# Moving a last copy across a stage boundary, swapping two small steps, and letting the last bank of a feed-forward lag five blocks

## The chip, the cores and the metric

The kernel runs on one core of a Trainium2 chip. The metric is the device time of one execution in microseconds (us); lower is better. Times of before come from three runs and one profiled execution.

## The reference, cut to what matters

One block of a perceiver on 16 batches of 64 tokens (1024 tokens, 512 channels) with a context of 16 x 1601 rows:

```
x = x + xattn(layernorm(x), ctx)      # 16 heads of 32, softmax over 1601 context rows
x = x + attn(layernorm(x))            # 16 heads of 32, 64 tokens per batch, alibi bias
h = square(relu(layernorm(x) @ W_fc.T))        # 512 -> 2048
y = h @ W_proj.T                               # 2048 -> 512
x = x + (spikes of a neuron driven by y in 5 steps) / 5
```

Every product is made in three matmul passes (high x high, low x high, high x low), where a float32 value is split into a high part that ScalarE rounds and a low part, the difference, that VectorE makes.

## The kernel before, in words

There are three stages, each a block of per-engine programs, with a boundary between them at which all engines meet: `prologue`, `cross_attention`, and `attention_and_feed_forward`. Within a stage the order on each engine is written out by hand, and semaphores join the engines. All DMAs are issued by SyncE (SP) on one queue.

**The prologue** (line 187) normalises x, turns it, and multiplies by Wq in eight query units n = 0 to 7 (four blocks of 128 output rows by two halves of 512 tokens), each 12 matmuls of 512 columns into one of four banks of `s_ps` (`q_bank[n % 4]`). ScalarE copies each unit to `xs` in `query(n)` (line 318), and SP stores it to HBM (`q_scratch`) in lines 235 to 238. ScalarE also splits the four quarters of the first batch's context, which VectorE completes. The last instruction of ScalarE is `query(7)`, the last of SP the store of unit 7.

**The cross-attention** (line 395) goes through 16 batches. SP first loads Wv (1024 KB), waits for all eight stores (`q_out`, line 517), loads the first batch's queries `q_sb` (128 KB), then the leftover context rows (`y_left`, 2304 KB), then the next batch's context. TensorE computes keys in units of 12 matmuls of 402 columns into a ring of three banks; ScalarE copies each to `k_sb[:, i % 2]`. The first scores (line 919), which read `q_sb`, follow the fifth key unit. The first write to `k_sb[:, 1]` is the copy of that fifth unit.

**The self-attention** is in the third stage. Its TensorE program is written out in lines 1770 to 1835. `qk(u)` makes 12 matmuls of 512 columns, into the same bank `ring_bank` for u from 10 on, so that each waits for ScalarE's copy of the one before (`qk_out`); `transposes(t, n)` turns half of the probabilities of token tile t into `t_bank` (4 matmuls), ScalarE's `copy` takes them out; `weigh(t)` multiplies them by the values (64 small matmuls), ScalarE's `high(t)` and VectorE's `low(t)` take the result out.

**The feed-forward** (loop at line 1837) has 48 blocks: 16 blocks of 128 hidden rows for each of three groups of token tiles, of 4, 2 and 2 tiles. In step m of the loop TensorE runs `hidden(m)` (12 matmuls, 256 columns in the last two groups), then `project(m - 3, ...)`, which is 3 matmuls of 512 columns per token tile. In the last group (blocks 32 to 47) the two tiles are parted: the first tile's bank is `project(m - 3)` and the last tile's bank is `project(m - 3 - LAG)`, with LAG = 3. So the loop goes on for 3 + LAG steps after the last `hidden`, and the last tile is finished LAG steps behind the first.

A block's values go through: `hidden(n)` on TensorE, relu on ScalarE (line 1435), square on VectorE (line 1515), the high part on ScalarE (`hidden_high`, line 1361), the low part on VectorE (`hidden_low`, line 1521), `project(n)` on TensorE. In the last group the high and low parts have six places (HS = 3 places of double width): the place of block n is that of block n - 6. `hidden_high(n)` therefore waits for `y_part`, which counts the blocks whose *last* bank is done:

```
        def h_before(n):
            return n - HS if n < ALL - FB + HS else n - 2 * HS
                act.wait_ge(sq_ok, n + 1)
                reached(act, y_part, h_before(n) + 1)
```

ScalarE's order in its step m is relu(m), `hidden_high(m - 1)`, and in steps 40 to 42 also `weights(19)` to `weights(21)` (line 1355), the high part of three weight blocks that are loaded anew; GpSimd makes their low parts (line 1319). VectorE's order is square(m), up to two neuron operations of earlier tiles, `hidden_low(m - 1)`. At the end VectorE runs six neuron operations for each of the last two tiles in a fixed interleaving (lines 1620 to 1633): four of the first tile (line 1489 once, 1493 three times), then the first of the last tile, which waits for the very last matmul, and so on; two stores of x end the program.

Of the kernel before, what the change touches and what calls it, by code (L numbers as in the profile page):

```python
# [8 lines left out]
ACT = mybir.ActivationFunctionType  # L9
# [6 lines left out]
P = 128  # L16
DC = D // P
MP = M + M % 2
TOK = B * N
TT = TOK // P  # L20
# [6 lines left out]
NBLK = H * DH // P  # L27
# [143 lines left out]
class Shared:  # L171


    def __init__(self, nc, ctx, context):
        sb = lambda n, s, d=F32: ctx.enter_context(nc.sbuf_tensor(n, s, d))
        sem = lambda n: ctx.enter_context(nc.semaphore(n))
        with ExitStack() as late:
            self.w_late = late.enter_context(nc.sbuf_tensor("w_late", [P, DC, D], F32))
        self.wk_s, self.wv_s = context.keep, sb("wv_s", [P, 2, DC, D], F32R)
        self.k_sb = sb("k_sb", [P, 2, MK])  # L180
        self.context = context
        self.y_in = [sem(f"y_in{q}") for q in range(KC)]
        self.y_hi_ok, self.y_lo_ok = sem("y_hi_ok"), sem("y_lo_ok")
        self.q_out = sem("q_out")


def prologue(nc, x, yT, wq, wk, q_dram, sh, ident, ones, s_ps):
# [4 lines left out]
    with ctx:  # L192
        sb = lambda n, s, d=F32: ctx.enter_context(nc.sbuf_tensor(n, s, d))
        sem = lambda n: ctx.enter_context(nc.semaphore(n))
        HALF = TT // 2
        HT = HALF * P
        NQ = NBLK * 2
# [3 lines left out]
        xs = sb("p_x", [P, TT, D])  # L201
# [9 lines left out]
        wq_in, wk_in = sem("p_wq_in"), sem("p_wk_in")  # L211
        ident_ok, ln_step, var_ok, root_ok, xn_ok = sem("p_ident"), sem("p_ln_step"), sem("p_var"), sem("p_root"), sem("p_xn")
        turned, xt_hi, xt_lo = sem("p_turned"), sem("p_xt_hi"), sem("p_xt_lo")
        q_ps, q_ok, wq_hi, wq_lo, wk_hi = sem("p_q_ps"), sem("p_q_ok"), sem("p_wq_hi"), sem("p_wq_lo"), sem("p_wk_hi")
        block = ctx.enter_context(nc.Block())

        def half_of(n):
# [2 lines left out]
        @block.sync  # L220
        def _(sp):
            def rows(n):
                at = slice(n * PAIR * P, (n + 1) * PAIR * P)
                sp.dma_start(xs[:, n * PAIR:(n + 1) * PAIR], x[at].rearrange("(t p) d -> p t d", p=P)).then_inc(x_in[n], 16)

            rows(0)
            rows(1)
            sp.dma_start(wq_raw[:], wq.rearrange("(c p) e -> p c e", p=P)).then_inc(wq_in, 16)
            rows(2)
            rows(3)  # L230
            sp.dma_start(wk_raw[:], wk.rearrange("(c p) e -> p c e", p=P)).then_inc(wk_in, 16)
# [3 lines left out]
            for n in range(NQ):  # L235
                half, i = half_of(n)
                sp.wait_ge(q_ok, n + 1)
# [67 lines left out]
        @block.scalar  # L305
        def _(act):
            def root(half):
                at = slice(half * HALF, (half + 1) * HALF)
                act.wait_ge(var_ok, half + 1)
                act.activation(ve[:, 1, at], ve[:, 0, at], ACT.Sqrt).then_inc(root_ok, 1)  # L310

            def high(half):
                for t in range(half * HALF, (half + 1) * HALF):
                    act.wait_ge(turned, t + 1)
                    act.activation(xnT[:, 0, :, t * P:(t + 1) * P],
                                   t_ps[t % 4][:].rearrange("p (c q) -> p c q", c=DC), ACT.Copy).then_inc(xt_hi, 1)

            def query(n):
                act.wait_ge(q_ps, n + 1)
                act.activation(xs[:, n, :], q_bank[n % 4], ACT.Copy).then_inc(q_ok, 1)  # L320
# [12 lines left out]
            query(0)  # L333
            query(1)
            query(2)
            high(1)
            context_high(0)
            query(3)
            for n in range(NBLK, NQ):
                if n - NBLK + 1 < KC:  # L340
                    context_high(n - NBLK + 1)
                query(n)

        @block.tensor
        def _(pe):
# [14 lines left out]
            def first_queries(units):  # L360

                pe.wait_ge(wq_hi, 1)
                pe.wait_ge(xt_hi, HALF)
                for n in units:
                    for c in range(DC):
                        product(n, c, 0, 0, start=(c == 0))
                pe.wait_ge(wq_lo, 1)
                for n in units:
                    for c in range(DC):
                        product(n, c, 1, 0)  # L370
                pe.wait_ge(xt_lo, HALF)
                for n in units:
                    for c in range(DC):
                        mm = product(n, c, 0, 1, stop=(c == DC - 1))
                    mm.then_inc(q_ps, 1)

            def queries(units):
                for n in units:
                    half, i = half_of(n)
                    pe.wait_ge(xt_lo, HALF * (half + 1))  # L380
                    if n >= 4:
                        pe.wait_ge(q_ok, n - 3)
                    three_passes(pe, q_bank[n % 4], lambda a, c: wq_s[:, a, c, i * P:(i + 1) * P],
                                 lambda a, c: xnT[:, a, c, half * HT:(half + 1) * HT]).then_inc(q_ps, 1)

            pe.wait_ge(ident_ok, 2)
            for n in range(WARM):
# [7 lines left out]
def cross_attention(nc, x, yT, y_left, v_left, q_dram, o_dram, wv, wp, bp, awq, sh, ident, ones, s_ps):  # L395
# [10 lines left out]
    with ctx:  # L406
# [73 lines left out]
        def _(sp):  # L480
# [33 lines left out]
                load_left(b + 1)  # L514

            sp.dma_start(wv_raw, wv.rearrange("(c p) e -> p c e", p=P)).then_inc(wv_in, 16)
            sp.wait_ge(sh.q_out, 16 * 2 * NBLK)
            load_q(0)
            sp.dma_start(left_rows, y_left).then_inc(left_in, 16)
# [52 lines left out]
        def _(act):  # L572
# [49 lines left out]
            def value_weights():  # L622
                act.wait_ge(wv_in, 16)
                act.activation(sh.wv_s[:, 0], wv_raw, ACT.Copy).then_inc(wv_hi, 1)

            def keys_phase(b, past=True):
                for c in range(KC):
                    key(b, 0, c)
                if not past:
                    value_weights()  # L630
                for i in range(1, NBLK):
                    key(b, i, 0)
                    score(b, i - 1, 0)
# [19 lines left out]
            def values_phase(b, more):  # L653
# [29 lines left out]
                else:  # L683
                    gather(2)

            keys_phase(0, False)
            values_phase(0, True)
            with act.Fori(1, B - 1) as b:
# [418 lines left out]
def attention_and_feed_forward(nc, x, attn_w, attn_b, wo, bo, alibi, w_ffn, context, x_sb, xnT, ident, out, s_ps):  # L1107
# [23 lines left out]
    LOADS = FB + MISSING * (len(GROUPS) - 1)  # L1131
    LEAD = 3
    HALF = OutputAndNorm.HALF
    AHEAD, LAG = 3, 3
    EARLY = 1
    QK = 2 * NBLK * 2
    ctx = ExitStack()
    with ctx:
# [499 lines left out]
        def _(pe):  # L1638
# [150 lines left out]
            transposes(0, 1)  # L1789
            scores(3)  # L1790
            qk(12)
            weigh(0)
            transposes(1, 0)
            qk(13)
            transposes(1, 1)
            qk(14)
            weigh(1)
            transposes(2, 0)
            qk(15)
            transposes(2, 1)  # L1800
            value(2)
# [112 lines left out]
```

## Time and profile before

| what | value |
|---|---|
| median of 3 runs | 1810.27 us (1810.23 to 1812.09) |
| the profiled execution's own time | 1810.56 us |
| its span | 1808.8 us |
| TensorE busy | 1791.4 us, 99% of the span |
| VectorE, ScalarE, GpSimd busy | 1306.2, 827.4, 898.4 us |
| granted TensorE clock, mean | 0.999 of full speed |

The span is what the profiler saw between the first and the last instruction; the execution's own time is 1.8 us longer. The end of a matmul in this profile is modelled, so a TensorE that is shown busy is not one at its peak. A timeline row gives start, duration, engine, line, operation and tiles, the count of merged instructions, and in brackets the idle time before it and what ended it. PEld is TensorE's weight load, which may run ahead of the matmul before it.

### The profile page before, as it was taken

The numbers are of one execution on the slowest core, as the hardware profiler recorded it, in microseconds if no ns is written. First come the engines' busy times: TensorE is split into PE (matmuls) and PEld (weight loads), VectorE is DVE, ScalarE is ACT, GpSimd is POOL, SyncE is SP. The second block draws the span as 40 slices with busy tenths as digits, with TensorE's granted clock in tenths as the row PEclk, the third lists the DMA queues.
The fourth block names the chain that finished last, engine by engine and source line by source line (L and its number), as shares of the span: only waits on it lengthen the run. The fifth ranks groups of instructions, "written<-read, shape, count | busy, mean of one in ns | idle before, by whom it ended". The sixth has DMA issues, their size and how long they took to land. (4 is left out here: it accounts for less than half of the span.)

```text
span 1808.8 us, 65801 instructions
## 1 busy us (share of the span) xinstructions
PE 1791.4 (99%) x28780; PEld 1557.7 (86%) x28780; DVE 1306.2 (72%) x1942; ACT 827.4 (46%) x982; POOL 898.4 (50%) x824
## 2 busy tenths in 40 slices
PE   8999999999999999999999999999999999999998
PEld 7979898989898989898989888888888887778887
DVE  6865959595969686877778686869696967574265
ACT  4634545454545454444445444545453524344232
POOL 0343737373737373737364646465555654344111
PEclk9999999999999999999999999999999999999999
DMA  6210202020202020202020201111020232123110
GB/s 254 112 54 3 84 3 83 4 83 3 84 3 83 4 83 3 83 3 84 3 83 9 78 21 66 42 45 65 22 83 3 76 114 69 26 91 107 37 59 24
DMA packets 43359, 101.20 MB, mean 56 GB/s; under 512 B 19120, under 2 KB 20656, under 8 KB 42960
## 3 DMA queue, kind: packets, MB, share of 16 engines
q1 hardware_dynamic: 43088, 96.88, 15.2%
q8 instruction: 256, 4.19, 0.9%
q14 instruction: 15, 0.12, 0.0%
HBM read 86.48 MB, written 8.29 MB: 52 GB/s over the span
## 5 line engine op out<-in xcount | busy, mean ns | idle before, releaser
L556 POOL TENSOR_TENSOR fold<-fold,prob 128x256 f32<-128x256 f32 x698 | 705.9, 1011 | 55.2
L114 PE MATMUL ring<-y_parts,w_keep 128*128 128x402 f32 (+1 forms) x3072 | 607.7, 351 | 1.5 <-PEq L192 1.4
L114 PEld LDWEIGHTS ring<-y_parts,w_keep 128*128 128x128 f32 x3072 | 551.4, 188 | 16.2 <-issue 3.1
L114 PE MATMUL ring<-wv_s,y_parts 128*128 128x512 f32 x2304 | 545.1, 395 | 0.0
L114 PEld LDWEIGHTS ring<-wv_s,y_parts 128*128 128x128 f32 x2304 | 430.7, 188 | 98.7
L550 POOL TENSOR_TENSOR fold<-prob 128x256 f32<-128x256 f32 x64 | 80.4, 1256 | 623.4 <-ACT prob L610 623.4
L579 ACT ACTIVATE k_sb<-ring 128x402 f32<-128x402 f32 (+1 forms) x256 | 129.4, 506 | 362.3 <-PE ring L114 362.3
L770 DVE TENSOR_TENSOR prob<-prob,peak_rows 128x1024 f32<-128x1024 f32 (+1 forms) x192 | 261.7, 1416 | 1.6
L604 ACT ACTIVATE prob<-s_ps 128x1536 f32<-128x1536 f32 (+1 forms) x128 | 200.0, 1562 | 127.8 <-PE s_ps L919 127.8
L735 DVE TENSOR_TENSOR fold<-fold,prob 128x512 f32<-128x512 f32 x192 | 173.0, 901 | 79.6 <-ACT prob L604 73.9
L610 ACT ACTIVATE prob<-prob 128x1024 f32<-128x1024 f32 (+1 forms) x192 | 210.9, 1125 | 7.4 <-DVE prob L770 5.1
L919 PEld LDWEIGHTS s_ps<-q_sb,k_sb 32*64 32x64 f32 x13312 | 156.2, 130 | 37.5 <-issue 37.3
L919 PE MATMUL s_ps<-q_sb,k_sb 32*64 32x64 f32 x13312 | 173.9, 231 | 0.0
L788 DVE TENSOR_TENSOR y_parts<-y_raw,y_parts 128x1608 fp32r<-128x1608 f32 (+1 forms) x60 | 123.8, 2084 | 35.7 <-ACT y_parts L615 35.7
L587 ACT ACTIVATE v_sb<-ring 128x512 f32<-128x512 f32 x96 | 57.4, 598 | 193.1 <-PE ring L114 193.1
L728 DVE TENSOR_TENSOR fold<-prob 128x512 f32<-128x512 f32 x64 | 52.8, 825 | 128.3 <-ACT prob L604 128.3
L615 ACT ACTIVATE y_parts<-y_raw 128x1608 fp32r<-128x1608 f32 (+1 forms) x60 | 92.4, 1540 | 32.8 <-PE ring L114 32.8
L938 PEld LDWEIGHTS small_ps<-prob,v_sb 128*32 128x32 f32 (+1 forms) x6344 | 91.5, 110 | 16.6 <-issue 16.6
L938 PE MATMUL small_ps<-prob,v_sb 128*32 128x64 f32 (+1 forms) x6344 | 101.4, 220 | 0.0
L707 DVE COPY v_sb<-ring 128x512 f32<-128x512 f32 x96 | 65.0, 677 | 15.5 <-PE ring L114 15.5
L762 DVE COPY peak<-peak 32x8 f32<-32x8 f32 x192 | 63.0, 328 | 6.2
L1319 POOL TENSOR_TENSOR y_parts<-f_raw,y_parts 128x1024 fp32r<-128x1024 f32 x12 | 30.1, 2519 | 73.7 <-ACT y_parts L1355 73.5
(214 smaller groups left out, 1622.2 us busy)
## 6 DMA issues: line engine op xcount, KB each, us to landing
y_raw<-yT SPq DMA_DIRECT2D x48, 804.0 KB, 7.1
y_raw<-yT SPq DMA_DIRECT2D x16, 792.0 KB, 9.9
f_raw<-w_ffn SPq DMA_DIRECT2D x22, 512.0 KB, 3.6
v_sb<-y_left SPq DMA_DIRECT2D x1, 2304.0 KB, 11.3
v_sb<-v_left SPq DMA_DIRECT2D x16, 130.0 KB
p_x<-x SPq DMA_DIRECT2D x4, 512.0 KB, 6.5
q_scratch<-p_x SPq DMA_DIRECT2D x8, 256.0 KB, 2.1
q_sb<-q_scratch SPq DMA_DIRECT2D x16, 128.0 KB, 9.2
```

The costliest lines, as they stand in the source:

```text
L114: mm = pe.matmul(out, left(a, c), right(b, c), start=(c == 0 and n == 0), stop=(c == DC - 1 and n == 2))
L550: pool.tensor_tensor(acc, prob[:, i, 0, :], prob[:, i, 1, :], ALU.add).then_inc(sum_step, 1)
L556: pool.tensor_tensor(acc[0:m], acc[0:m], prob[0:m, i, t, :], ALU.add).then_inc(sum_step, 1)
L579: act.activation(k_sb[:, i % 2, at:at + w], bank(unit)[:, 0:w], ACT.Copy).then_inc(act_out, 1)
L604: act.activation(prob[:, i, a:z, :].rearrange("p t (g q) -> p t g q", g=HB), s_ps[:, :, 0:(z - a) * N].rearrange("p g (t q) -> p t g q", q=N),
L610: act.activation(piece(i, n), piece(i, n), ACT.Exp, scale=SCALE).then_inc(exp_ok, 1)
L615: act.activation(y.part(0, q), y.quarter(q), ACT.Copy).then_inc(y_hi_ok, 1)
L735: dve.tensor_tensor(wide(i), wide(i), prob[:, i, t:t + 2, :], ALU.max).then_inc(tree, 1)
L770: dve.tensor_tensor(piece(i, n), piece(i, n), row(n), ALU.subtract).then_inc(sub_ok, 1)
L788: dve.tensor_tensor(y.part(1, q), y.quarter(q), y.part(0, q).bitcast(F32), ALU.subtract).then_inc(y_lo_ok, 1)
L919: mm = pe.matmul(s_ps[side * N:(side + 1) * N, g, (t - a) * N:(t - a + 1) * N], k_sb[rows, i % 2, at:at + N], q_sb[rows, i, :], start=True ...
L938: pe.matmul(at[g * DH:(g + 1) * DH, 0:N], v_sb[0:m, t, (HB * i + g) * DH:(HB * i + g + 1) * DH], prob[0:m, i, t, g * N:(g + 1) * N], start ...
```

## The change

It does three things. The copy of query unit 7 leaves the prologue: ScalarE makes it as its first instruction of the cross-attention, into the unused second half of `k_sb`; SP stores it there, behind the load of Wv; and ScalarE waits for all stores before it writes that half of `k_sb`. In the self-attention `transposes(1, 0)` is put ahead of `weigh(0)` and `transposes(2, 0)` ahead of `weigh(1)`. LAG in the feed-forward becomes 5.

```
@@ class Shared
-        self.q_out = sem("q_out")
+        self.q_out, self.q_ps, self.q_ok = sem("q_out"), sem("p_q_ps"), sem("p_q_ok")
+        self.last_q = self.k_sb[:, 1, 0:TT // 2 * P]
@@ prologue, SP  (q_ps and q_ok are sh.q_ps and sh.q_ok from here on)
-            for n in range(NQ):
+            for n in range(NQ - 1):
                 half, i = half_of(n)
-                sp.wait_ge(q_ok, n + 1)
+                sp.wait_ge(sh.q_ok, n + 1)
                 sp.dma_start(q_dram[:, i, half * HT:(half + 1) * HT], xs[:, n]).then_inc(sh.q_out, 16)
@@ prologue, ScalarE
             for n in range(NBLK, NQ):
                 if n - NBLK + 1 < KC:
                     context_high(n - NBLK + 1)
-                query(n)
+                if n < NQ - 1:
+                    query(n)
@@ cross_attention, SP
             sp.dma_start(wv_raw, wv.rearrange("(c p) e -> p c e", p=P)).then_inc(wv_in, 16)
+            sp.wait_ge(sh.q_ok, 2 * NBLK)
+            sp.dma_start(q_dram[:, NBLK - 1, TOK // 2:], sh.last_q).then_inc(sh.q_out, 16)
             sp.wait_ge(sh.q_out, 16 * 2 * NBLK)
             load_q(0)
@@ cross_attention, ScalarE
+            def last_queries():
+                act.wait_ge(sh.q_ps, 2 * NBLK)
+                act.activation(sh.last_q, s_ps[:, NBLK - 1, :], ACT.Copy).then_inc(sh.q_ok, 1)
+
             def keys_phase(b, past=True):
                 for c in range(KC):
                     key(b, 0, c)
                 if not past:
                     value_weights()
+                    act.wait_ge(sh.q_out, 16 * 2 * NBLK)
                 for i in range(1, NBLK):
...
+            last_queries()
             keys_phase(0, False)
@@ attention_and_feed_forward
-    AHEAD, LAG = 3, 3
+    AHEAD, LAG = 3, 5
@@ attention_and_feed_forward, TensorE
             qk(12)
+            transposes(1, 0)
             weigh(0)
-            transposes(1, 0)
             qk(13)
             transposes(1, 1)
             qk(14)
+            transposes(2, 0)
             weigh(1)
-            transposes(2, 0)
             qk(15)
```

## Rows read from the trace of the kernel before

**Rows 1.** The page: busy time by engine.

```profile
PE 1791.4 (99%) x28780; PEld 1557.7 (86%) x28780; DVE 1306.2 (72%) x1942; ACT 827.4 (46%) x982; POOL 898.4 (50%) x824
```

**Rows 2.** Timeline at the boundary behind the prologue: start, duration, engine, line, what.

```profile
23.23 13.86 PE L114 MATMUL s_ps<-p_xnT,p_wq 128*128 128x512 f32 x60
...
37.12 0.60 ACT L320 ACTIVATE p_x<-s_ps 128x512 f32<-128x512 f32 x1 [2.12 <-PE s_ps L114]
...
38.52 11.23 PE L114 MATMUL ring<-y_parts,w_keep 128*128 128x402 f32 x60 [1.44 <-PEq L192]
```

**Rows 3.** Timeline at the boundary behind the cross-attention, TensorE.

```profile
1481.62 3.06 PE L987 MATMUL s_ps<-w_keep,y_parts 128*128 128x512 f32 x12
...
1484.99 3.04 PE L114 MATMUL ring_bank<-w_keep,y_parts 128*128 128x512 f32 x12 [0.30 <-PEq L406]
```

**Rows 4.** DMA issues from 38 to 60 us: KB each, us to landing; then the first scores.

```profile
v_sb<-xwv SPq DMA_DIRECT2D x1, 1024.0 KB, 5.7
q_scratch<-p_x SPq DMA_DIRECT2D x1, 256.0 KB, 2.1
q_sb<-q_scratch SPq DMA_DIRECT2D x1, 128.0 KB, 4.9
...
49.68 1.25 PE L919 MATMUL s_ps<-q_sb,k_sb 32*64 32x64 f32 x96
```

**Rows 5.** Timeline of the self-attention, TensorE.

```profile
1545.56 3.05 PE L114 MATMUL ring_bank<-xnT,y_parts 128*128 128x512 f32 x12
1548.54 0.26 PE L1718 MATMUL o_banks<-y_raw 64*32 64x64 f32 x4
...
1549.33 0.66 PE L1701 MATMUL t_bank<-ident,sa_chain 128*128 128x128 f32 x4
1549.74 3.03 PE L114 MATMUL ring_bank<-xnT,y_parts 128*128 128x512 f32 x12
1552.60 0.60 PE L1701 MATMUL t_bank<-ident,sa_chain 128*128 128x128 f32 x4
1553.63 3.02 PE L114 MATMUL ring_bank<-xnT,y_parts 128*128 128x512 f32 x12 [0.43 <-ACT kT L1330]
```

**Rows 6.** Timeline of the feed-forward's last blocks and end.

```profile
1793.17 1.57 PE L1760 MATMUL s_ps<-y_parts,f_h 128*128 128x512 f32 x6
...
1794.35 0.65 PEld L1760 LDWEIGHTS s_ps<-f_w,f_h 128*128 128x128 f32 x3
...
1794.84 0.42 ACT L1361 ACTIVATE f_h<-y_raw 128x256 fp32r<-128x256 f32 x1 [0.77 <-PE s_ps L1760]
...
1795.29 0.43 DVE L1521 TENSOR_TENSOR f_h<-y_raw,f_h 128x256 fp32r<-128x256 f32 x1 [0.74 <-ACT f_h L1361]
...
1798.74 2.23 PE L1760 MATMUL s_ps<-f_w,f_h 128*128 128x512 f32 x9
...
1801.03 0.68 DVE L1489 TENSOR_SCALAR y_raw<-s_ps 128x512 f32<-128x512 f32 x1
```

**Rows 7.** Timeline: a projection that had waited for VectorE's low part.

```profile
1741.21 0.41 DVE L1521 TENSOR_TENSOR f_h<-y_raw,f_h 128x256 fp32r<-128x256 f32 x1
...
1741.67 1.23 PEld L1760 LDWEIGHTS s_ps<-w_keep,f_h 128*128 128x128 f32 x6 [0.63 <-DVE f_h L1521]
```

**Rows 8.** Feed-forward steps 40 to 43: ScalarE's and GpSimd's weights, projections; line 1319.

```profile
1774.27 1.05 ACT L1355 ACTIVATE f_w<-f_raw 128x1024 fp32r<-128x1024 f32 x1
...
1775.40 5.46 POOL L1319 TENSOR_TENSOR f_w<-f_raw,f_w 128x1024 fp32r<-128x1024 f32 x2 [35.59 <-ACT f_w L1355]
...
1779.78 0.86 PE L1760 MATMUL s_ps<-f_w,f_h 128*128 128x512 f32 x3
1780.05 1.09 DVE L1521 TENSOR_TENSOR f_h<-y_raw,f_h 128x256 fp32r<-128x256 f32 x1
...
1781.77 0.53 PEld L1760 LDWEIGHTS s_ps<-y_parts,f_h 128*128 128x128 f32 x3
...
L1319 POOL TENSOR_TENSOR f_w<-f_raw,f_w x3: 2402/2588/2916, 1775.4 to 1781.0; 128x1024 fp32r<-128x1024 f32 x3
```

More of the change, by code:

```diff
@@ L183, in __init__ @@
         self.y_hi_ok, self.y_lo_ok = sem("y_hi_ok"), sem("y_lo_ok")
-        self.q_out = sem("q_out")
+        self.q_out, self.q_ps, self.q_ok = sem("q_out"), sem("p_q_ps"), sem("p_q_ok")
+        self.last_q = self.k_sb[:, 1, 0:TT // 2 * P]
 def prologue(nc, x, yT, wq, wk, q_dram, sh, ident, ones, s_ps):
@@ L213, in prologue @@
         turned, xt_hi, xt_lo = sem("p_turned"), sem("p_xt_hi"), sem("p_xt_lo")
-        q_ps, q_ok, wq_hi, wq_lo, wk_hi = sem("p_q_ps"), sem("p_q_ok"), sem("p_wq_hi"), sem("p_wq_lo"), sem("p_wk_hi")
+        wq_hi, wq_lo, wk_hi = sem("p_wq_hi"), sem("p_wq_lo"), sem("p_wk_hi")
         block = ctx.enter_context(nc.Block())
@@ L234, in _ @@
                 sp.dma_start(y.raw[:, DC * at:DC * (at + w)], yT[0, :, DC * at:DC * (at + w)]).then_inc(sh.y_in[q], 16)
-            for n in range(NQ):
+            for n in range(NQ - 1):
                 half, i = half_of(n)
-                sp.wait_ge(q_ok, n + 1)
+                sp.wait_ge(sh.q_ok, n + 1)
                 sp.dma_start(q_dram[:, i, half * HT:(half + 1) * HT], xs[:, n]).then_inc(sh.q_out, 16)
@@ L318, in query @@
             def query(n):
-                act.wait_ge(q_ps, n + 1)
-                act.activation(xs[:, n, :], q_bank[n % 4], ACT.Copy).then_inc(q_ok, 1)
+                act.wait_ge(sh.q_ps, n + 1)
+                act.activation(xs[:, n, :], q_bank[n % 4], ACT.Copy).then_inc(sh.q_ok, 1)
             def context_high(q):
@@ L341, in _ @@
                     context_high(n - NBLK + 1)
-                query(n)
+                if n < NQ - 1:
+                    query(n)
         @block.tensor
@@ L374, in first_queries @@
                         mm = product(n, c, 0, 1, stop=(c == DC - 1))
-                    mm.then_inc(q_ps, 1)
+                    mm.then_inc(sh.q_ps, 1)
             def queries(units):
@@ L381, in queries @@
                     if n >= 4:
-                        pe.wait_ge(q_ok, n - 3)
+                        pe.wait_ge(sh.q_ok, n - 3)
                     three_passes(pe, q_bank[n % 4], lambda a, c: wq_s[:, a, c, i * P:(i + 1) * P],
-                                 lambda a, c: xnT[:, a, c, half * HT:(half + 1) * HT]).then_inc(q_ps, 1)
+                                 lambda a, c: xnT[:, a, c, half * HT:(half + 1) * HT]).then_inc(sh.q_ps, 1)
             pe.wait_ge(ident_ok, 2)
@@ L516, in _ @@
             sp.dma_start(wv_raw, wv.rearrange("(c p) e -> p c e", p=P)).then_inc(wv_in, 16)
+            sp.wait_ge(sh.q_ok, 2 * NBLK)
+            sp.dma_start(q_dram[:, NBLK - 1, TOK // 2:], sh.last_q).then_inc(sh.q_out, 16)
             sp.wait_ge(sh.q_out, 16 * 2 * NBLK)
@@ L624, in value_weights, with last_queries @@
                 act.activation(sh.wv_s[:, 0], wv_raw, ACT.Copy).then_inc(wv_hi, 1)
+            def last_queries():
+                act.wait_ge(sh.q_ps, 2 * NBLK)
+                act.activation(sh.last_q, s_ps[:, NBLK - 1, :], ACT.Copy).then_inc(sh.q_ok, 1)
             def keys_phase(b, past=True):
@@ L630, in keys_phase @@
                     value_weights()
+                    act.wait_ge(sh.q_out, 16 * 2 * NBLK)
                 for i in range(1, NBLK):
@@ L684, in values_phase @@
                     gather(2)
+            last_queries()
             keys_phase(0, False)
@@ L1133, in attention_and_feed_forward @@
     HALF = OutputAndNorm.HALF
-    AHEAD, LAG = 3, 3
+    AHEAD, LAG = 3, 5
     EARLY = 1
@@ L1791, in _ @@
             qk(12)
+            transposes(1, 0)
             weigh(0)
-            transposes(1, 0)
             qk(13)
@@ L1796, in _ @@
             qk(14)
+            transposes(2, 0)
             weigh(1)
-            transposes(2, 0)
             qk(15)
```

## The prediction

> **What bounds the kernel now.** I read the page first, then the timeline at the three places that the change touches. TensorE is busy 99% of the span [rows 1] and no other engine over 72%, so only what opens or closes an idle stretch of TensorE counts, besides what follows its last matmul. The first such place is the boundary behind the prologue: the last query matmul ends at 37.09 (23.23 + 13.86) and the next stage's first starts at 38.52, 1.44 us idle. ScalarE's copy of query unit 7 lies inside that gap, 37.12 to 37.72, and SP's store follows it [rows 2]. The second is the self-attention around `weigh(0)`, the third the last 16 blocks of the feed-forward and the end [rows 5 to 8].
>
> **A, the copy and store of unit 7.** Removed from ahead of the boundary: one 0.60 us copy and one store. TensorE is then the last engine to arrive. The boundary behind the cross-attention shows that case: last matmul ends 1484.68, next starts 1484.99, idle 0.30 [rows 3]. So A gains 1.44 - 0.30 = 1.14 us. Bounds: 0.84 (a gap of 0.6 stays, twice the other boundary's) to 1.3 (a gap near 0.1); I take 1.14, from the nearest row. Added behind the boundary: the same copy, first on ScalarE, which otherwise has nothing until the first key unit; nothing waits behind it. On SP the store and the wait for it now stand between the Wv load and `load_q(0)`. The Wv load lands 5.7 us after its issue, a store alone 2.1, and `q_sb`, issued behind Wv, landed after 4.9 [rows 4]. If the store waits out Wv it has landed by 5.7 + 2.1 = 7.8 us after the boundary, and `q_sb`, with an empty queue, some 2.1 later, at about 10. TensorE wants it at 49.68 - 38.52 = 11.2 us [rows 2, 4]. So it costs 0, with little over 1 us of cover; it is a rival below. The leftover rows and the next context are issued up to 6 us later than before on the same queue; they are read by ScalarE and VectorE after the first scores, and TensorE's wait for them lies further still; 0. ScalarE's new wait stands where ScalarE comes some 10 us after the boundary, when the stores are in: 0.
>
> The Trainium skill (DMA: Bandwidth & Descriptors, section Queues, rings and completion order) says that descriptors of one queue are consumed in ring order and that a semaphore increment lands only after every earlier write of that DMA engine. By it the store lands behind Wv and not after 2.1 us. The landing of `q_sb` at 4.9, when Wv was ahead of it, agrees.
>
> **B, the two swaps.** The same instructions, another order. Now: `qk(12)` starts 1545.56, the weighing 1548.54, the turn 1549.33, `qk(13)` 1549.74, 4.18 us in all. In the new order the turn follows a `qk`, which takes 2.86 us as at `qk(13)` (1549.74 to 1552.60); the weighing starts when the turn's 0.60 are over, and the next `qk` 0.79 after it as the turn did: 4.25 [rows 5]. So +0.07 at the dearest; a turn that is overlapped at its end by the next matmul would make it -0.1. Two swaps: 0, bounds -0.2 to +0.2. What the swap brings, a turned half that ScalarE copies 0.9 us sooner, nobody waits for; what TensorE does wait for is ScalarE's copy of the `qk` bank, 0.43 us ahead of `qk(14)` [rows 5], and that bank and the single turn that covers its copy are as before.
>
> **C, LAG 5.** The number of matmuls is the same: two blocks' last-bank projections leave steps 38 and 39 and come behind the old end. The dependence is not the same. `hidden_high(n)` waits for the last bank of block n - 6, which is now run in step n - 6 + 3 + 5 = n + 2, at that step's very end; the first bank of block n is wanted in step n + 3. With LAG 3 it was step n, three steps ahead. So the chain *end of a projection, high part, low part, next projection* now turns once a step. Its length from rows: the matmul ends at e = 1793.17 + 1.57 = 1794.74, the high part starts 0.10 later (1794.84), the low part 0.45 after that (1795.29), lasts 0.43 [rows 6], and a weight load started 0.05 behind a low part that it waited for [rows 7]. Sum: e + 1.03.
>
> *Steps 48, 49, 50* have no `hidden`; each first-bank projection (blocks 45, 46, 47) follows directly on the last-bank projection for which its own high part waits. Without the wait its weight load starts at 1794.35 = e - 0.39 [rows 6]. So each is delayed by 1.03 + 0.39 = 1.42 us, and three by 4.26. Bounds: 1.32 each if the first 0.10 is nothing, 1.55 each if TensorE picks up again slower, 4.0 to 4.7 in all.
>
> The Trainium skill (Perfetto Trace Analysis, section Tensor Engine Instruction) says that the end of a matmul in the profile is computed and not observed. By it the 0.10 is soft; with 0 in its place the three would cost 4.0. No row here shows a matmul's true end.
>
> *Steps 41 to 47* (blocks 38 to 44) have a `hidden` between. After e = 1779.78 + 0.86 = 1780.64 the next projection's weight load starts at 1781.77, e + 1.13 [rows 8]. The chain is ready at e + 1.03: hidden, by 0.10 us. I take 0 for these; if the chain is longer by 0.2 to 0.4, seven steps cost 0.7 to 2.1.
>
> *GpSimd in that stretch.* A low part that starts under GpSimd's line 1319 does not end before it: the second of its operations ended at 1775.40 + 5.46 = 1780.86, and the low part begun at 1780.05 took 1.09 and ended at 1781.14, 0.28 behind [rows 8]. Now nobody waits for that; with LAG 5 TensorE does. `weights(19)` to `weights(21)` stand behind `hidden_high(39)`, (40), (41), so they now start some 0.45 after the end of steps 41, 42, 43; GpSimd follows 1.13 after ScalarE's start (1774.27 to 1775.40) and takes 2.40 (the shortest of the three) [rows 8]: it ends at 0.45 + 1.13 + 2.40 = 3.98. A step is 1.13 to the next projection's weight load, 1.57 for the six matmuls of both projections [rows 6] and, as an estimate, a tenth for the load's lead: 2.8. So GpSimd ends 1.18 into the next step; the low part ends at 1.46, the weight load starts at 1.51 instead of 1.13: 0.4 late. Then the step is longer (3.2), the second operation ends 0.8 into the following one and the chain's own 1.03 rules; the third is as the first. Two delays: +0.8, bounds 0 (GpSimd early by half a microsecond) to 1.6 (three at 0.5).
>
> *The end.* The first tile's bank is done two blocks (1.4 us) sooner relative to TensorE's end, so VectorE's four operations on it are over before it. But VectorE's first operation on the last tile starts at 1801.03 already, and the last matmul ends at 1798.74 + 2.23 = 1800.97 [rows 6]: it waits for TensorE and not for those four. From there the eight operations stand in the same order. Gain 0.0 to 0.1; I take 0.
>
> **The sum.** -1.14 + 0 + 4.26 + 0.8 = +3.9 us. Against the profiled execution's own 1810.56 that is 1814.5; the median of the runs shown is 0.3 lower, so I predict 1814.2. Its own bounds: -1.3 - 0.2 + 4.0 + 0 = +2.5 to -0.84 + 0.2 + 4.7 + 1.6 = +5.7.
>
> **The rivals.**
> 1. *Not slower.* Only A acts: the three waits at the end don't open because a high part is let go earlier than I read (the place would have to be free one projection sooner). Price: 1810.3 - 1.1 = 1809.1. It decides where C's sum is under 1.14, that is under 0.4 us per wait. Against it: the wait names block n - 6 and `y_part` counts last banks alone. 0.10.
> 2. *The seven covered steps open too*: the margin of 0.10 us is within the softness of a modelled end. About 0.2 each, +1.4: 1815.6. For it: the margin; against: TensorE's pick-up after VectorE was 0.05 in the one row. 0.17.
> 3. *The boundary keeps its gap*: another engine's arrival or the jump to new code holds it at 1.4; +1.1: 1815.3. Against: the 0.30 of the other boundary. 0.08.
> 4. *The first scores wait for `q_sb`*: store 7.8 us, then a load of 4.9 as measured in a busy queue, 12.7 against 11.2: +1.5, 1815.7. 0.05.
> 5. *A's and C's terms both smaller*, the chain overlapped better than the rows let see, 1 us per wait and nothing from GpSimd: +1.9, 1812.2. 0.05.
>
> **How the numbers follow.** The forecast has 0.55. A measurement of this kernel can tell about 0.2%, 3.6 us, from no change: 1813.9 is the line, and the forecast lies just beyond it. Of its 0.55 I give 0.31 above and 0.24 below. Slower: 0.31 + 0.17 + 0.08 + 0.05 = 0.61; faster by over 3.6 us would need rival 1 and a gain that I don't see: 0.02; the rest, 0.37, within. The range takes the forecast's bounds nearly whole, reaches over rivals 2 to 4, and leaves out rival 1 and rival 5: 1812.5 to 1816.8.
>
> **What would show it.** At the boundary: TensorE's first key matmul with 0.3 idle instead of 1.44, ScalarE's copy behind it, `q_sb` landed before the first scores, which show no wait for a DMA. In the self-attention: the same 0.43 ahead of `qk(14)`. In the last group: ScalarE's high parts waiting for TensorE's line 1760 once a step; a low part stretched under GpSimd and TensorE waiting for it twice; after the last `hidden` three waits of TensorE on VectorE's line 1521 with about 1 us of idle each; VectorE's line 1489 for the last tile right behind the last matmul. The prediction is wrong if those three waits are missing, if the seven covered steps show idle of their own, or if the boundary still has over 1 us.

## The result, and the profile after

| | before | changed |
|---|---|---|
| median of 16 runs each, same chip | 1810.37 us (1810.06 to 1813.58) | 1814.10 us (1813.75 to 1816.68) |
| ratio, with its 95% interval | | 1.0020 (1.0013 to 1.0028) |
| profiled execution's own time | 1810.56 us | 1814.45 us |
| its span | 1808.8 us | 1812.6 us |

The changed kernel is 3.7 us slower; the interval of the ratio makes this 2.4 to 5.1 us. The forecast of 1814.2 was 0.1 us above the measured median. The two profiled spans differ by 3.8 us, so the profile shows what the medians show, and the mean granted clock is 0.999 in both.

First the page's busy time by engine, of the changed kernel (to hold against [rows 1]).

```profile
PE 1793.6 (99%) x28780; PEld 1558.9 (86%) x28780; DVE 1305.5 (72%) x1942; ACT 827.8 (46%) x982; POOL 898.6 (50%) x824
```

The counts are the same to the instruction: nothing was added to any engine's work. TensorE is still shown busy 99% of the span. A loss of 4 us in 1810 can't be seen here, and TensorE's busy time even rose by 2.2 us. The places that the change touches have to be read one by one.

**The boundary behind the prologue** (answers to [rows 2]). Timeline of the changed kernel: start, duration, engine, line, what; in brackets the idle time before it. Line numbers of the changed kernel are up to 10 higher than those of before; ScalarE's copy is now line 632.

```profile
37.56 0.39 SPq L518 DMA_DIRECT2D v_sb<-xwv  x1
...
37.58 0.60 ACT L632 ACTIVATE k_sb<-s_ps 128x512 f32<-128x512 f32 x1 [2.38 <-PEq L193]
37.61 11.24 PE L114 MATMUL ring<-y_parts,w_keep 128*128 128x402 f32 x60 [0.32 <-PEq L193]
38.21 0.33 SPq L520 DMA_DIRECT2D q_scratch<-k_sb  x1
...
43.89 0.69 SPq L490 DMA_DIRECT2D q_sb<-q_scratch  x1
...
48.78 1.25 PE L929 MATMUL s_ps<-q_sb,k_sb 32*64 32x64 f32 x96
```

TensorE is idle for 0.32 us instead of 1.44, and ScalarE's copy of unit 7 now runs beside its first key matmuls. The price is on SP's queue. The view of the DMA issues from 37 to 60 us (KB each, us from issue to landing; answers to [rows 4]) has it:

```profile
v_sb<-xwv SPq DMA_DIRECT2D x1, 1024.0 KB, 5.6
...
q_scratch<-k_sb SPq DMA_DIRECT2D x1, 256.0 KB, 5.7
q_sb<-q_scratch SPq DMA_DIRECT2D x1, 128.0 KB, 2.7
```

The store took 2.1 us when it was issued ahead of the Wv load. Behind it, it takes 5.7 and lands when Wv has. Only then does SP issue the load of `q_sb` (43.89), which lands at 43.89 + 2.7 = 46.6. The first scores start at 48.78 and their row names no wait: 2.2 us of cover, the time between the landing and the first use, are left.

**The self-attention** (answers to [rows 5]). Timeline of TensorE in the changed kernel:

```profile
1544.66 3.05 PE L114 MATMUL ring_bank<-xnT,y_parts 128*128 128x512 f32 x12
1547.55 0.60 PE L1711 MATMUL t_bank<-ident,sa_chain 128*128 128x128 f32 x4
1548.08 0.26 PE L1728 MATMUL o_banks<-y_raw 64*32 64x64 f32 x4
...
1548.87 3.05 PE L114 MATMUL ring_bank<-xnT,y_parts 128*128 128x512 f32 x12
...
1552.79 3.01 PE L114 MATMUL ring_bank<-xnT,y_parts 128*128 128x512 f32 x12 [0.43 <-ACT kT L1340]
```

From `qk(12)` to `qk(13)` it is 4.21 us, against 4.18. The 0.43 us ahead of `qk(14)` stand as before. Over both swaps, from `qk(12)` to `qk(15)`, it is 12.29 us (1544.66 to 1556.95) against 12.23 (1545.56 to 1557.79).

**The feed-forward.** The waits view of the changed kernel from 1760 us to the end (engine, buffer, line, what it waited for: us in total, times, longest):

```profile
ACT f_h L1371 <- PE s_ps L1770: 20.1, 10, 3.2
DVE f_h L1531 <- ACT f_h L1371: 16.7, 10, 2.6
...
PEld s_ps L1770 <- DVE f_h L1531: 5.0, 5, 1.5
...
PE s_ps L1770 <- DVE f_h L1531: 3.1, 3, 1.0
```

The same view of before has ScalarE's high part waiting for TensorE once (0.8 us), VectorE's low part once (0.7 us), and no row of TensorE waiting for a low part.

So the loop from a projection through ScalarE and VectorE back to TensorE is closed in ten steps, and TensorE's weight load is late in five of them. Two of the five lie under GpSimd. Timeline of the changed kernel, steps 40 to 43 (answers to [rows 8]):

```profile
1777.34 2.41 POOL L1329 TENSOR_TENSOR f_w<-f_raw,f_w 128x1024 fp32r<-128x1024 f32 x1 [38.22 <-ACT f_w L1365]
...
1777.72 0.86 PE L1770 MATMUL s_ps<-f_w,f_h 128*128 128x512 f32 x3
...
1779.12 0.90 DVE L1531 TENSOR_TENSOR f_h<-y_raw,f_h 128x256 fp32r<-128x256 f32 x1 [1.10 <-ACT f_h L1371]
...
1780.08 0.53 PEld L1770 LDWEIGHTS s_ps<-y_parts,f_h 128*128 128x128 f32 x3 [0.31 <-DVE f_h L1531]
...
1780.88 0.86 PE L1770 MATMUL s_ps<-f_w,f_h 128*128 128x512 f32 x3
...
1782.87 0.53 PEld L1770 LDWEIGHTS s_ps<-y_parts,f_h 128*128 128x128 f32 x3
...
1786.02 0.53 PEld L1770 LDWEIGHTS s_ps<-y_parts,f_h 128*128 128x128 f32 x3 [0.26 <-DVE f_h L1531]
```

The low part lasts 0.90 us instead of 0.43 and ends at 1780.02, 0.27 behind GpSimd's end (1777.34 + 2.41 = 1779.75). The load behind it starts 1780.08 - (1777.72 + 0.86) = 1.50 us after the projection before it ended. In the following step, where GpSimd has ended early enough, it is 1782.87 - 1781.74 = 1.13, and one step later late again.

The other three stand behind the last `hidden`. Timeline of the changed kernel, the end (answers to [rows 6]):

```profile
1791.80 1.55 PE L1770 MATMUL s_ps<-y_parts,f_h 128*128 128x512 f32 x6
1793.44 0.42 ACT L1371 ACTIVATE f_h<-y_raw 128x256 fp32r<-128x256 f32 x1 [2.14 <-PE s_ps L1770]
...
1793.89 0.42 DVE L1531 TENSOR_TENSOR f_h<-y_raw,f_h 128x256 fp32r<-128x256 f32 x1 [1.87 <-ACT f_h L1371]
...
1794.37 0.97 PE L1770 MATMUL s_ps<-f_w,f_h 128*128 128x512 f32 x3 [1.02 <-DVE f_h L1531]
...
1794.94 0.65 PEld L1770 LDWEIGHTS s_ps<-y_parts,f_h 128*128 128x128 f32 x3
...
1797.06 0.97 PE L1770 MATMUL s_ps<-f_w,f_h 128*128 128x512 f32 x3 [1.02 <-DVE f_h L1531]
...
1799.76 0.96 PE L1770 MATMUL s_ps<-f_w,f_h 128*128 128x512 f32 x3 [1.02 <-DVE f_h L1531]
...
1802.63 2.22 PE L1770 MATMUL s_ps<-f_w,f_h 128*128 128x512 f32 x9
1804.89 0.69 DVE L1499 TENSOR_SCALAR y_raw<-s_ps 128x512 f32<-128x512 f32 x1 [1.27 <-PE s_ps L1770]
```

Read the first four rows as one chain: the projection ends at 1793.35, the high part starts 0.09 later, the low part 0.45 behind that, TensorE 0.48 behind that. That is 1.02 us in which the array has nothing, by the modelled end, three times over. VectorE's first operation on the last tile, which started at 1801.03 before, starts at 1804.89.

### The profile page after: what moved, and what is told of

It reads as the page before. It is cut to its first block and busy times, and to the rows that moved or that the text cites. A ratio compares the mean times of both kernels' runs of the same rounds, so it can differ in the third digit from the quotient of the medians.

```text
span 1812.6 us, 65802 instructions
## 1 busy us (share of the span) xinstructions
PE 1793.6 (99%) x28780; PEld 1558.9 (86%) x28780; DVE 1305.5 (72%) x1942; ACT 827.8 (46%) x982; POOL 898.6 (50%) x824
```

## The experiments

Each kernel ran on the same chip as the kernel before, and its differences are against that; three chips were used, on which the kernel before had medians of 1810.85, 1810.13 and 1810.61 us. Each interval of a ratio reaches some 1.7 us to either side, so most single differences below are not resolved from nothing by the times alone; the trace must say the rest.

### One part at a time

**Only the moved copy** (part A): the changed kernel with the two swaps undone and LAG = 3.

> The kernel before with part A alone (unit 7 copied and stored behind the boundary). My theory: TensorE's idle at the boundary goes from 1.44 to about 0.3, and the time falls by 1.1 us (1809.2 where before is 1810.3). Rival (the gain is given back later in the cross-attention because q_sb or the leftover rows come late): same time as before, with a wait of TensorE or ScalarE on a DMA.

```
-    AHEAD, LAG = 3, 5
+    AHEAD, LAG = 3, 3
-            transposes(1, 0)
             weigh(0)
+            transposes(1, 0)
...
-            transposes(2, 0)
             weigh(1)
+            transposes(2, 0)
```

Measured: 1809.60 us, -1.25 against before (ratio 0.9992, 0.9983 to 1.0001). Timeline at the boundary:

```profile
37.22 4.10 PE L114 MATMUL ring<-y_parts,w_keep 128*128 128x402 f32 x21 [0.32 <-PEq L193]
```

The gap is 0.32 us again, 1.12 less than before.

**Only the swaps** (part B), on the kernel before.

> The kernel before with the two swaps (part B) alone. My theory: no change, within 0.2 us; in the trace qk(12) to qk(13) takes 4.2 us as before and TensorE still waits 0.43 us ahead of qk(14). Rival (the swaps cost or bring something that A hid in the whole change): more than 0.3 us to either side, in the idle time of TensorE between qk(12) and value(2).

```
-            weigh(0)
             transposes(1, 0)
+            weigh(0)
...
-            weigh(1)
             transposes(2, 0)
+            weigh(1)
```

Measured: 1810.54 us, +0.4 (1.0002, 0.9993 to 1.0011), not to be told from nothing. TensorE's timeline:

```profile
1545.59 3.05 PE L114 MATMUL ring_bank<-xnT,y_parts 128*128 128x512 f32 x12
...
1549.79 3.05 PE L114 MATMUL ring_bank<-xnT,y_parts 128*128 128x512 f32 x12
...
1553.71 3.01 PE L114 MATMUL ring_bank<-xnT,y_parts 128*128 128x512 f32 x12 [0.43 <-ACT kT L1330]
```

4.20 us from `qk(12)` to `qk(13)` and the same 0.43 ahead of `qk(14)`: the trace gives the first swap 0.02 us, and both together 0.05 (`qk(15)` starts at 1557.87, 12.28 after `qk(12)`).

**Only LAG 5** (part C), on the kernel before, run on two chips.

> The kernel before with LAG = 5 alone. My theory: +5.0 us against before: three waits behind the last hidden block, 1.42 each, and two of about 0.35 to 0.4 under GpSimd's weights. Rival (A did not bring its 1.1, and C costs less): +3.8.

```
-    AHEAD, LAG = 3, 3
+    AHEAD, LAG = 3, 5
```

> LAG = 5 alone once more, on the same chip as the next kernel, because the two waits under GpSimd are worth less than the difference between chips. Both theories: +4.5 to +5.0 against before.

Measured: 1815.40 us, +4.55 (1.0026, 1.0015 to 1.0036), and on the other chip 1815.46, +4.85 (1.0027, 1.0017 to 1.0036). So part C alone makes the whole loss and more, and A gives some of it back: -1.25 + 4.7 is 3.5, measured 3.7. The end in the first run's timeline:

```profile
1792.40 1.55 PE L1760 MATMUL s_ps<-y_parts,f_h 128*128 128x512 f32 x6
1794.34 0.42 ACT L1361 ACTIVATE f_h<-y_raw 128x256 fp32r<-128x256 f32 x1 [2.43 <-PE s_ps L1760]
...
1795.27 0.98 PE L1760 MATMUL s_ps<-f_w,f_h 128*128 128x512 f32 x3 [1.32 <-DVE f_h L1521]
```

The three waits are there (the later two 1.03 and 1.02 us), but the first is 1.32 us and not 1.02: ScalarE starts 0.39 us after the modelled end of the projection. The changed kernel doesn't have these 0.3 us, so the parts that it has add up to 3.2 rather than 3.5, by medians that are each known to some 1.7 us. The late start comes back below.

### Is it the lag, or the places of the high and low parts?

The forecast put the loss on the six places: block n must wait for block n - 6's last bank. Its rival is that the longer lag costs by itself, for instance since two blocks' projections are run at the end. Four kernels tell these apart.

**LAG 4.** With it the wait is for a projection one step earlier.

> The kernel before with LAG = 4. The high part of block n then waits for a projection in step n + 1, not n + 2. My theory: the chain of 1.03 us has a whole step more to cover it, so no wait under GpSimd, and behind the last hidden block at most 0.03 each: within 0.2 us of before. Rival (the lag itself costs, by a longer tail of last-bank projections): a third to a half of the cost of LAG 5, +0.7 to +2.5.

```
-    AHEAD, LAG = 3, 3
+    AHEAD, LAG = 3, 4
```

Measured: 1810.78 us, -0.1 (1.0000, 0.9991 to 1.0009). Its waits view from 1760 us:

```profile
ACT f_h L1361 <- PE s_ps L1760: 10.9, 10, 1.4
DVE f_h L1521 <- ACT f_h L1361: 9.7, 10, 1.4
```

ScalarE waits for a projection in ten steps, as with LAG 5, but there is no row in which TensorE waits for the low part. The loop is closed, with a step of slack in it. What one step of lag costs is nothing that these runs can see; what the second costs is all.

**LAG 5 and the last bank first.** In the three steps that have no `hidden`, the last tile's projection goes ahead of the first tile's, so that the three matmuls of the first bank run while ScalarE and VectorE work.

> LAG = 5 alone, and in the steps behind the last hidden block the last bank's projection is put ahead of the first bank's, so that 0.69 us (step 48) and 1.39 us (steps 49, 50) of TensorE's work lie between the projection that frees a place and the one that needs it. My theory: the three waits shrink from 1.02 idle each to about 0.3 to 0.4, 0 and 0; the time is +5.0 - 3.5 = +1.5 us against before (first bank done 0.7 later, which VectorE hides). Rival (the waits come from the length of ScalarE's and VectorE's queues, not from the freed place): no change against LAG = 5.

```
-    AHEAD, LAG = 3, 3
+    AHEAD, LAG = 3, 5
...
+                if n >= ALL:
+                    project(n - AHEAD - LAG, BANKS[-1][1:])
                 if AHEAD <= n < ALL - FB + AHEAD:
                     project(n - AHEAD, BANKS[(n - AHEAD) // FB])
                 elif ALL - FB + AHEAD <= n < ALL + AHEAD:
                     project(n - AHEAD, BANKS[-1][:1])
-                if n >= ALL - FB + AHEAD + LAG:
+                if ALL - FB + AHEAD + LAG <= n < ALL:
                     project(n - AHEAD - LAG, BANKS[-1][1:])
```

Measured: 1812.21 us, +1.4 (1.0007, 0.9998 to 1.0016), 3.2 less than LAG 5 as it is on the same chip. Of the three waits one is left:

```profile
1795.61 0.98 PE L1760 MATMUL s_ps<-f_w,f_h 128*128 128x512 f32 x3 [0.62 <-DVE f_h L1521]
```

The same matmuls, lagging as far, in another order: the 3 us were the order of the dependence and not the lag. The wait that is left is 0.62 us where 0.3 to 0.4 was expected; ScalarE's high part ahead of it has the same 2.43 us of idle as with LAG 5 alone (it starts at 1794.68), and 0.39 behind the modelled end of the sixth matmul (1792.74 + 1.55, as six take above), so the late start is there again, and it makes up the excess.

**LAG 5 and eight places** (HS 4). The memory on chip has no room for a fourth double place beside three raw weight buffers, so one of those goes.

> LAG = 5 alone, with eight places for the hidden values of the last group instead of six (HS = 4); to make room, two raw weight buffers instead of three. Block n then waits for block n - 8, in step n, as with LAG 3 and six places. My theory: all five waits go and the time is that of before, within 0.3 us, if the missing raw buffer costs nothing. Rival (the cost is that of a longer tail): +4 or more stays.

```
-    RAW, WIDE, OWN, HELD, AS, HS, HB = 3, 6, 5, 13, 2, 3, 4
+    RAW, WIDE, OWN, HELD, AS, HS, HB = 2, 6, 5, 13, 2, 4, 4
-    AHEAD, LAG = 3, 3
+    AHEAD, LAG = 3, 5
```

Measured: 1809.32 us, -0.8 (0.9995, 0.9986 to 1.0004); its profiled execution was one of the longer ones, 1811.76 us, so only its waits and the times between rows of it are read here. No matmul waits for a low part in the last group. It came out below the kernel before, which LAG 3 with HS 3 doesn't explain. The time from the first projection to the `hidden` of step 37, all ahead of the changed lag, is 0.7 us shorter than before. There the second group's projection of [rows 7], which waited for its low part, starts at 1743.03 and doesn't wait. Before, this projection's weight load waits 0.63 us. In the run with seven places, the next one, HS and RAW stay 3; there the load waits 0.63 us as before, so it is not the lag that takes the wait away. HS and RAW were changed together and not tried apart, so which of them does it is open.

**LAG 5 and seven places.** To keep three raw buffers, the seventh place of the last group is put into an unused end of the context's parts; block n waits for block n - 7.

> LAG = 5 alone, with a seventh place for the hidden values of the last group in an unused end of the context tensor. Block n waits for block n - 7, in step n + 1, as with LAG 4 and six places. My theory: as LAG 4, within 0.2 us of before. Rival: as LAG 5 with six places, +4 or more.

```
-            at = w * (n // HS % 2) if n // FB == len(GROUPS) - 1 else 0
-            return h_s[:, n % HS, :, at:at + w]
+            at, slot = 0, n % HS
+            if n // FB == len(GROUPS) - 1:
+                k = (n - (ALL - FB) + SEVENTH) % 7
+                if k == 6:
+                    return context.parts[:].rearrange("p s c m -> p s (c m)")[:, :, WIDE * 2 * D:WIDE * 2 * D + w]
+                at, slot = w * (k // 3), (k + 2) % 3
+            return h_s[:, slot, :, at:at + w]
...
-            return n - HS if n < ALL - FB + HS else n - 2 * HS
+            return n - HS if n < ALL - FB + HS else n - 7
...
-    AHEAD, LAG = 3, 3
+    AHEAD, LAG = 3, 5
     EARLY = 1
+    SEVENTH = 0
```

Measured: 1810.31 us, +0.2 (1.0003, 0.9994 to 1.0012). One more place takes away LAG 5's loss. No row of its waits view from 1760 us has TensorE waiting for a low part, and VectorE's first operation on the last tile starts 0.48 us earlier than before, of which 0.45 were already there at the `hidden` of step 37, ahead of the changed lag:

```profile
1800.55 0.69 DVE L1495 TENSOR_SCALAR y_raw<-s_ps 128x512 f32<-128x512 f32 x1 [1.28 <-PE s_ps L1766]
```

That settles the rival: by the trace the lag by itself costs nothing, and it brings nothing either; by the medians neither is more than about 2 us, against the 4.7 of six places.

### What the two waits under GpSimd are worth

GpSimd makes only 64 of the 1024 columns of the low parts of the weight blocks 19 to 21, and all else is as with LAG 5 alone. The other 960 columns of these low parts are left out of the computation; the matmuls are all run.

> LAG = 5 alone, and GpSimd makes only the first 64 of 1024 columns of the low part for weight blocks 19 to 21 (that part of the computation is left out). My theory: the stretched low parts and TensorE's two waits of about 0.3 in steps 43 and 45 go, the three behind the last hidden block stay: 0.7 us faster than LAG = 5 alone, about +4.3 against before. Rival (the two waits are the chain's own length and GpSimd only stands beside it): no change against LAG = 5 alone.

```
-                pool.tensor_tensor(w[:, 1], f_raw[:, n % RAW, :], w[:, 0].bitcast(F32), ALU.subtract).then_inc(w_lo, 1)
+                m = 64 if n >= 19 else 2 * D
+                pool.tensor_tensor(w[:, 1, 0:m], f_raw[:, n % RAW, 0:m], w[:, 0, 0:m].bitcast(F32),
+                                   ALU.subtract).then_inc(w_lo, 1)
```

Measured: 1814.66 us, +4.5 (1.0024, 1.0014 to 1.0033). This was another chip than that of LAG 5 alone, and the kernel before differs between those two by 0.7 us, as much as is to be found. So both were run again side by side.

> LAG = 5 with the short low parts of weight blocks 19 to 21, beside LAG = 5 alone on one chip. My theory: 0.6 to 0.7 us faster than LAG = 5 alone. Rival (TensorE's lost time there is made up further on, where it would have waited anyway): within 0.2 us of it.

Measured: 1814.65 us, +4.0 (1.0022, 1.0013 to 1.0031), against +4.85 of LAG 5 alone on that chip: 0.8 us less by the medians, 0.5 by the profiled spans (1812.8 against 1813.3). Its timeline, at the place where the low part took 0.90:

```profile
1779.68 0.43 DVE L1523 TENSOR_TENSOR f_h<-y_raw,f_h 128x256 fp32r<-128x256 f32 x1 [1.10 <-ACT f_h L1363]
1780.26 0.53 PEld L1762 LDWEIGHTS s_ps<-y_parts,f_h 128*128 128x128 f32 x3
```

The low part takes 0.43 us and the load behind it has no wait. The mechanism is shown. Its size rests on the traces, 0.37 and 0.36 us for the two late loads; the difference of 0.5 to 0.8 us between the two kernels agrees, but is less than the 1.7 us to which a difference of medians is known.

### Finishing the first tile whole

In the last chain VectorE interleaves the two tiles' operations, so some of the first tile's stand between the last tile's. If the first tile is done early enough, it could be finished whole, and the last tile's six could run in one go behind the last matmul.

> Part A, both swaps, LAG 3, and at the end VectorE does all six operations of the first tile before those of the last. My theory: the first tile's bank is done only 2.8 us before the last matmul, six dependent operations of 0.72 take 4.3, so the last tile starts 1.5 late and the end comes 0.6 later than with the interleaving: -1.2 + 0.6 = -0.6 against before. Rival (the interleaving itself costs, the order is better at any lag): -1.8.

```
-    AHEAD, LAG = 3, 5
+    AHEAD, LAG = 3, 3
-            last(0)
-            last(0)
-            last(0)
-            last(0)
-            last(1)
-            last(0)
-            last(1)
-            last(0)
-            last(1)
+            for _ in range(OPS):
+                last(0)
             dve.wait_ge(spike, first + before[0] + 1)
             dve.sem_inc(done, 1)
-            last(1)
-            last(1)
-            last(1)
+            for _ in range(OPS):
+                last(1)
```

With A, the swaps and LAG 3: 1810.34 us, -0.3 (0.9998, 0.9989 to 1.0007), less than the -1.25 of A alone. Its timeline:

```profile
1797.78 2.23 PE L1762 MATMUL s_ps<-f_w,f_h 128*128 128x512 f32 x9
1798.01 2.87 DVE L1503 SCALAR_TENSOR_TENSOR y_raw<-s_ps,y_raw 128x512 f32<-128x512 f32 x4
...
1801.76 0.69 DVE L1499 TENSOR_SCALAR y_raw<-s_ps 128x512 f32<-128x512 f32 x1 [0.15 <-DVE x_sb L1501]
```

The last matmul ends at 1800.01, but VectorE takes the last tile up only at 1801.76, 1.75 us late, because the first tile isn't finished. From the last matmul's end to VectorE's last it is 6.1 us, against 5.3 before.

> The changed kernel with eight places for the hidden values (two raw weight buffers) and the six operations of the first tile before those of the last. My theory: no wait of TensorE for a freed place; the first tile's bank is done 4.1 us before the last matmul, so its six operations (4.3) lie beside TensorE and only the last tile's six remain, 4.5 us behind the last matmul instead of 5.3: -1.2 (A) - 0.8 (as eight places alone) - 0.75 = -2.8 us against before, faster than both kernels. Rival (the end is set by the store of x and not by VectorE, or the new order costs): -2.0.

The same edit of VectorE's order on the changed kernel with eight places (HS 4, RAW 2, LAG stays 5). Measured: 1808.25 us, -2.4 (0.9987, 0.9978 to 0.9996), halfway between the -2.8 that was expected and the rival's -2.0. It is faster than the kernel before, by 0.7 to 4.0 us by the interval, and about 6 below the changed kernel, by the two differences (2.4 + 3.7). Its timeline:

```profile
1791.10 0.86 PE L1762 MATMUL s_ps<-f_w,f_h 128*128 128x512 f32 x3
...
1796.65 2.22 PE L1762 MATMUL s_ps<-f_w,f_h 128*128 128x512 f32 x9
...
1799.24 0.69 DVE L1499 TENSOR_SCALAR y_raw<-s_ps 128x512 f32<-128x512 f32 x1 [0.15 <-DVE x_sb L1501]
...
1802.87 0.69 DVE L1501 SCALAR_TENSOR_TENSOR x_sb<-y_raw,x_sb 128x512 f32<-128x512 f32 x1
```

The projections of the steps without `hidden` follow at 1.38 us a step (the next starts at 1792.48) with no wait between. The last tile is taken up at 1799.24, 0.37 behind the last matmul's end (1798.87), and the last operation ends at 1803.56, 4.7 us behind it. In the changed kernel that stretch is 1804.85 to 1810.15, 5.3 us. So here the longer lag does pay, 0.6 us by the trace, once there are places enough to hold the blocks and an order of VectorE that uses the early tile. About 1.1 of the rest is A, and some 0.7 the wait that vanished with eight places (the stretch up to the `hidden` of step 37 is again 0.7 shorter).

## Why the prediction was right

The sign, the place and the mechanism were as forecast, and the size came out to 0.1 us. That last agreement is partly luck: the forecast made part C 0.4 us dearer than the trace shows it, the measured difference is 0.1 to 0.2 us more than the terms of the trace, and its interval is 2.7 us wide. The terms, against what they measured:

| term | predicted | shown |
|---|---|---|
| A, the boundary | -1.14 | gap 1.44 to 0.32, -1.12; A alone -1.25 by medians, not resolved from 0 |
| A, `q_sb` behind the store | 0, cover a little over 1 | 0, cover 2.2 |
| B, the swaps | 0 (-0.2 to +0.2) | +0.06 for both, +0.05 with the swaps alone; their median not resolved from 0 |
| C, steps 48 to 50 | +4.26 | three waits; 1.30 each, +3.9 |
| C, the seven covered steps | 0 | 0 but for GpSimd's two |
| C, GpSimd | +0.8 in two steps | two steps, 0.37 + 0.36 = +0.7 |
| the end | 0 | 0 |
| sum | +3.9 | +3.6; medians +3.7, profiled spans +3.8 |

**A.** "TensorE is then the last engine to arrive" holds: the other boundary's 0.30 was the right neighbour. The store did not wait out Wv and then take its own 2.1 us on top; it landed 0.7 after Wv (43.9 against 43.2), so 7.8 was 1.5 too late and the cover larger. The Trainium skill (DMA: Bandwidth & Descriptors, section Queues, rings and completion order) has the descriptors of one queue consumed in ring order on each DMA engine; the landings agree, 5.7 us for a store that alone took 2.1. By position, the changed kernel's first key matmul came 0.9 us earlier than before (37.61 against 38.52) and not 1.12, since its query matmuls had started 0.16 later in that execution and ended 0.19 later (37.28 against 37.09). Such differences of a start are in every comparison of two profiles, and this one is most of what parts the sum of the terms from the difference of the spans.

**C, the chain.** The forecast had e + 1.03 for the end of the chain, added from rows of before in none of which this chain had held anything up; all three waits of the changed kernel are 1.02. This is where the prediction earned its result: ScalarE's 0.10, 0.45 between the high and low part, 0.43 of the low part, 0.05 of pick-up were each visible while the chain was still hidden.

**C, the price of a wait.** This is the term that was mis-sized most, by 0.4 us in all. "Each is delayed by 1.03 + 0.39 = 1.42": the load does start 1.41 us later than it would have. But a projection whose load has waited has an idle array ahead of it, and its next load follows after 1794.94 - 1794.37 = 0.57 us, where before, without waits, loads of that shape follow each other every 0.69 (1794.35, 1795.04). That gives 0.12 or so back. Step to step it is 2.69 us (1794.37 to 1797.06) against the 1.38 of the last experiment: 1.3 each, and 3.9 in all instead of 4.26.

**C, the covered steps.** The margin of 0.10 held: in step 47 the low part ends at 1791.49 and the load starts at 1791.68, with no wait in its row. Rival 2, which had 0.17, did not happen. It was near: LAG 4, which differs by one step of slack, shows what a margin that doesn't hang on a tenth looks like.

**C, GpSimd.** The load was forecast at 1.51 us after the projection's end instead of 1.13, twice, with the second of three operations too early to matter. The trace has 1.50, 1.13, 1.49. The forecast rounded the difference of 0.38 up to 0.4, twice.

**The position of the whole.** From the `hidden` of step 37 (1763.67, before 1764.36) to the first operation on the last tile the changed kernel lost 4.55 us: it was 0.69 ahead there and is 3.86 behind at the end. The terms say 3.9 + 0.7 = 4.6.

**Rival 1** ("not slower") fell with the three waits; **rivals 3 and 4** with the 0.32 us gap and the scores' row without a wait; **rival 5** with 1.3 us a wait. What no run settles is how far the result is beyond 0.2%: the ratio is 1.0020, and its interval lies on both sides of the line at 1813.9 us that the forecast had drawn.

## What to carry to other kernels

When a consumer is let lag behind, count the buffers against the lag: the lag is free up to the point at which the release of the oldest buffer stands right ahead of its next use on the same engine, and from there every step costs the whole round trip through the other engines (here 1.3 us a step, nothing at LAG 4, nothing with one more buffer). Steps with other work between hide that round trip, so the cost appears first where this work has run out, at the end of the loop. And a copy that is the last thing an engine does ahead of a barrier can go behind it, if the buffer it reads stays alive and the transfers that follow have a microsecond or two to spare; here the gap at the boundary shrank by 1.1 us, in every trace with part A that was read.

## What the runs showed that was not expected

- **One high part of ScalarE starts late, and it is always the same one.** With LAG 5 on the kernel before (alone, with short low parts, and with the last bank first), ScalarE's high part of block 45 started 0.39 us after the modelled end of the projection (1794.34 against 1793.95); in the changed kernel the same step shows 0.09, and so do all the later ones. It makes the first of the three waits 1.3 us instead of 1.0. The Trainium skill (Perfetto Trace Analysis, section Tensor Engine Instruction) says that a matmul's end in the profile is computed, so this row alone can't say whether the matmuls ended later or ScalarE was slower to start. Other runs can. With LAG 4 the high part of block 45 waits for a projection one step earlier, and it is again 0.39 behind it, while the next one is 0.09 behind its own (1793.81 against 1793.72):

```profile
1789.31 1.57 PE L1760 MATMUL s_ps<-y_parts,f_h 128*128 128x512 f32 x6
...
1791.27 0.42 ACT L1361 ACTIVATE f_h<-y_raw 128x256 fp32r<-128x256 f32 x1 [1.37 <-PE s_ps L1760]
```

  With seven places it is 0.39 too (1790.45 against 1790.06). In the kernel before this high part follows ScalarE's relu and waits for no matmul, and there it starts 0.36 us after the relu's start (1790.53, 1790.89) where its neighbours start 0.28 after theirs. So the delay goes with this one operation of ScalarE and not with the matmuls ahead of it. It is missing in the changed kernel, in part A alone, in A with LAG 3 and the new order, and in LAG 5 with eight places; with A, eight places and the new order the start is again 0.36 behind the relu's. What causes it, and why it comes and goes with edits elsewhere, is open.
- **The end of a blocked low part.** A low part that VectorE begins while GpSimd runs its 1024 columns ends 0.27 us behind GpSimd (1780.02 against 1779.75), as in before (0.28). When GpSimd has only 64 columns the low part lasts its usual 0.43 us.
- **A kernel's level differs between chips.** The same kernel before had medians of 1810.13, 1810.61 and 1810.85 us on three chips, with 30 to 32 runs each. The effect of GpSimd, under 1 us, could only be looked for between two kernels on one chip.
- **Eight places made something else faster**: 0.7 us in the second group of the feed-forward, where the wait of [rows 7] went away. It was not sought, and it makes a good part of what the best version gains.
